# A four-layer block on one core: rebuilt prologue, one-tile statistics, reordered quantised expert

## What is computed

```
x = L0_attn_hidden_states                       # 2 x 512 x 512
x = x + LN(_L0_attn_ref(LN(x), ...))            # selective scan (below)
x = x + LN(_L0_ffn_ref(LN(x), ...))             # 4-bit weights, 1376 wide, gate * sigmoid(gate) * up
x = x + LN(_L1_attn_ref(LN(x), ...))            # attention within a token, 32 heads of 16
x = x + LN(_L1_ffn_ref(LN(x), ...))             # mixture of experts with a shared expert

# _L0_attn_ref, D_IN = 1024, N = 16 states, R = 32:
proj = h @ W_in.T; x, gate = proj[..., :D_IN], proj[..., D_IN:]
x = silu(causal_conv4(x) + conv_b)
ts, Bm, Cm = rms-normed parts of x @ W_x.T      # 32, 16, 16
dt = softplus(ts @ W_dt.T + b_dt)
state = state * exp(dt * A) + (dt * x) * B      # per token, channel and state
y = sum(state * C) + x * D
return (y * silu(gate)) @ W_out.T
```

## Time and profile before

| | us |
|---|---|
| median of 3 runs (lowest, highest) | 844.3 (842.31, 845.25) |
| the profiled execution, device time | 844.68 |
| its span in the trace | 842.8 |
| PE busy | 692.8 (82%) |
| DVE busy | 691.4 (82%) |
| POOL busy | 493.8 (59%) |
| ACT busy | 460.0 (55%) |
| mean granted TensorE clock | 0.904 |

### The profile page before, as it was taken

The page is one execution under the profiler, slowest core; times in us unless marked ns, Lnnn a source line. Parts: engine busy times, 40 slices in busy tenths (PEclk is TensorE's granted clock), DMA queues, the critical chain, the costliest instruction groups (busy, mean ns, idle before and its releaser), DMA issues. The chain is left out here.

```text
span 842.8 us, 8287 instructions
## 1 busy us (share of the span) xinstructions
PE 692.8 (82%) x2732; PEld 320.0 (38%) x2732; DVE 691.4 (82%) x700; ACT 460.0 (55%) x772; POOL 493.8 (59%) x258
## 2 busy tenths in 40 slices
PE   5989679998777879366648868997999999999993
PEld 4533123332222323011112223433444546787882
DVE  5779899999999999979999989997265564586668
ACT  3556687797655765856555434765334346323421
POOL 1319999989999999999998920210002005340151
PEclk9999879999968999756858979999999999999998
DMA  9224312331535524533127029870040030000011
GB/s 289 49 74 158 118 37 95 126 124 65 185 103 182 168 75 138 176 124 113 38 100 222 28 76 236 227 210 18 1 150 1 0 100 2 1 0 1 1 51 50
DMA packets 40945, 82.39 MB, mean 98 GB/s; under 512 B 6711, under 2 KB 8160, under 8 KB 40648
## 3 DMA queue, kind: packets, MB, share of 16 engines
q1 hardware_dynamic: 40904, 81.87, 31.0%
HBM read 70.65 MB, written 11.21 MB: 97 GB/s over the span
## 5 line engine op out<-in xcount | busy, mean ns | idle before, releaser
L2142 POOL TENSOR_TENSOR dbu<-rep_du,bc 128x1024 f32<-128x1024 f32 x128 | 299.6, 2366 | 2.3 <-ACT rep_du L1837 1.4
L1708 ACT ACTIVATE psum<-rep_dt,aneg 128x512 f32<-128x512 f32 x256 | 166.2, 682 | 125.2 <-DVE hc L1115 104.8
L1104 DVE TENSOR_TENSOR_SCAN psum<-psum,dbu 128x1024 f32<-128x1024 f32 x87 | 198.8, 2285 | 10.2 <-ACT psum L1708 9.7
L881 PE MATMUL psum<-hc,stk 128*32 128x512 f32 x512 | 87.5, 762 | 58.8 <-POOL hc L2151 30.4
L1115 DVE TENSOR_TENSOR hc<-psum,bc 128x1024 f32<-128x1024 f32 x87 | 106.5, 1224 | 3.4 <-PE psum L881 0.4
L2151 POOL TENSOR_TENSOR hc<-hc,bc 128x1024 f32<-128x1024 f32 x41 | 96.8, 2360 | 8.6 <-DVE hc L1104 8.5
L1104 DVE TENSOR_TENSOR_SCAN hc<-psum,dbu 128x1024 f32<-128x1024 f32 x41 | 93.5, 2281 | 4.7 <-PE psum L881 2.8
L658 PE MATMUL psum<-xf_hi,gu_hi 128*128 128x512 f16 x176 | 67.4, 383 | 1.5 <-ACT sg L1982 1.0
L658 PE MATMUL psum<-xf_hi,gu_lo 128*128 128x512 f16 x176 | 67.2, 382 | 0.0
L658 PE MATMUL psum<-xf_lo,gu_hi 128*128 128x512 f16 x176 | 67.2, 382 | 0.0
L873 PE MATMUL psum<-u,diag 128*32 128x512 f32 x128 | 24.6, 851 | 42.3 <-DVE u L1131 22.9
(11 more groups left out here) (256 smaller groups left out, 1444.5 us busy)
## 6 DMA issues: line engine op xcount, KB each, us to landing
rep_dt<-rep_scratch SPq DMA_DIRECT2D x60, 256.0 KB, 3.3
rep_du<-rep_scratch SPq DMA_DIRECT2D x60, 256.0 KB, 4.2
cw<-c_scratch SPq DMA_DIRECT2D x11, 768.0 KB, 9.4
qw<-qgu_in SPq DMA_DIRECT2D x11, 512.0 KB, 5.3
bc<-bc_scratch SPq DMA_DIRECT2D x16, 256.0 KB, 4.8
...
```

The costliest lines, as they stand in the source:

```text
L881: last = pe.matmul(y_rows(k), stk[:], hc[:, (i + k // 2) % HCS, k % 2, :], start=False, stop=(s == GN - 1))
L1104: dve.tensor_tensor_scan(h, a, dbu[:, i % DBS].rearrange("p e t -> p (e t)"), 0.0, ALU.mult, ALU.add)\
L1708: last = act.activation(psum[:, 2 * (i % 2) + e, :], rep_dt[:, cc % 2, k, :], ACT.Exp, scale=aneg[:, k, c, n:n + 1])
L2142: pool.tensor_tensor(dbu[:, i % DBS], rep_du[:, cc % 2, k:k + 2, :], bc[:, n, :].unsqueeze(1).broadcast_to([P, 2, L]), ALU.mult).then_inc( ...
```

## The change

There are five parts.

1. **Prologue.** PE runs 12 products of the identity with itself as soon as the identity is loaded, 3 after each of the first three turned tiles and 8 after the last; their result is not used. The projection weights `w_x` come in four DMAs and not two. The Silu table is loaded before the first `conv_tap`, the Ln/Exp table before `square`. `ssm_first` stands behind chunks 4, 5 and 6 (three of them) and behind the last chunk (five). `ms_part` stands ahead of both halves of gate 0. dt of chunk 1 goes to PSUM bank 3 (`dt_second`), ACT takes it in two passes (`dt1_log`, `dt1_pos`), and the rest is done in the loop at pair 2 (`second_steps`). Each spread row group of dt * x goes into a PSUM bank of its own; DVE makes the first `dbu` straight from two of them, and POOL starts with pair 1. The statistics `("ssm", 1)` move behind `normed_ssm(0)`, their root to pair 6, and all four tiles are normed on ACT in the loop.
2. **Side work.** Three gates instead of four are done before the loop, and the rest of `SIDE`'s first row moves by one. dt of chunk 2 is made two places later. The partial output product of tile 3 takes 7 channel chunks and not 6, so one is left for after the loop.
3. **Residual statistics** of sequence 0: `sums` one tile per pair at pairs 91 to 94, `squares` one per pair at 95 to 98, the root at 99 (before: two per pair, at 90, 91, 92 and 93, the root at 94).
4. **Quantised expert.** `unpack(1)` stands before the last `take_y`, `unpack(2)` behind `low_weights(1)`, and `add_partial` is interleaved in another way; on ACT the Silu table is loaded first and `high_weights(1)` stands before `whole(2)`. `high_turned` and `low_turned` for sequence 1 stand at the beginning of a chunk. The statistics `("out", 1)` move from the end of chunk 0 to behind `ffn_low(0, 1)`, those of `("ffn", 1)` from the end of chunk 4 to behind `ffn_low(0, 5)`.
5. **Waits.** Since POOL's first `times_b` is gone, all counts of `bmul_done` are one lower.

```diff
-SIDE = {(0, 1): [("gate", 0, 4)], (0, 2): [("gate", 0, 5)], (0, 3): [("gate", 0, 6)],
-        (1, 1): [("gate", 0, 7)], (1, 2): [("tr", "ssm", 1, 0), ("tr", "ssm", 1, 1)],
+SIDE = {(0, 1): [("gate", 0, 3)], (0, 2): [("gate", 0, 4)], (0, 3): [("gate", 0, 5)],
+        (1, 0): [("gate", 0, 6)], (1, 1): [("gate", 0, 7)], (1, 2): [("tr", "ssm", 1, 0), ("tr", "ssm", 1, 1)],
...
-DT_LATE = DC - 2
+DT_LATE = {0: 2, DC - 2: 1}
...
+            def keep_clock(n):
+
+                for _ in range(n):
+                    pe.matmul(psum[:, 0, 0:P], ident[:], ident[:], start=True, stop=True)
+
             pe.wait_ge(ld_ident, 16)
+            keep_clock(12)
             for t in range(NT):
                 turn("ssm", 0, t, xn)
+                keep_clock(3 if t < NT - 1 else 8)
...
+            def dt_second():
+                pe.matmul(psum[:, KH - 1, :], wdt[0:2 * R + 1, P:2 * P], ssmn[0:2 * R + 1, :], start=True, stop=True)\
+                    .then_inc(dt1_ready, 1)
...
-                if c >= 2:
-                    ssm_first(c - 2)
-            ssm_first(DC - 2)
+                if DC - 1 - SSM_EARLY <= c < DC - 1:
+                    ssm_first(c - DC + 1 + SSM_EARLY)
+            for c in range(SSM_EARLY, DC):
+                ssm_first(c)
+            pe.wait_ge(ld_const, 16 * 6)
+            ms_part(0)
             pe.wait_ge(ld_wg, 16)
             pe.wait_ge(xT_ready, 1)
             gate_half(0, 0, 0)
-            ssm_first(DC - 1)
-            pe.wait_ge(ld_const, 16 * 6)
-            ms_part(0)
             gate_half(0, 0, 1)
...
             dt_part(0)
-            dt_part(1)
-            gate_half(0, 1, 0)
+            dt_second()
             pe.wait_ge(sel_ready, 1)
             wait_taken(pe, ("dt", 0))
-            spread_half(dt_t, 0)
-            spread_half(dt_t, 1)
+            spread_dt_half(0)
             pe.wait_ge(du0_ready, 1)
-            for h in range(2):
-                pe.wait_ge(spread_dt[h], 2)
-                spread_half(du_t, h)
-            gate_half(0, 1, 1)
-            for c in range(2, GATES_FIRST):
+            spread_one(du_t, 0, psum[:, Y_BANK, :])
+            for k in range(1, KH):
+                spread_du(k)
+            pe.wait_ge(dt1_taken, 1)
+            spread_dt_half(1)
+            for c in range(1, GATES_FIRST):
                 gate_part(0, c)
...
+            dve.wait_ge(spread_done, 1)
+            dve.tensor_copy(rep_dt[:, 0, 1, 1:], psum[:, 1, 1:]).then_inc(spread_dt[0], 1)
+
+            wait_work(dve, ("spread", 1))
+            dve.wait_ge(ld_b[0][0], 16)
+            dve.tensor_tensor(dbu[:, 0], psum[:, Y_BANK:Y_BANK + 2, :],
+                              bc[:, 0, :].unsqueeze(1).broadcast_to([P, 2, L]), ALU.mult).then_inc(first_dbu, 1)
+
+            def second_steps():
+
+                dve.wait_ge(sp_ready, 2)
+                dve.wait_ge(spread_done, 2)
+                dve.tensor_tensor(dt_t[:], dt1_log[:], dt1_pos[:], ALU.add).then_inc(dt1_sum, 1)
+                dve.wait_ge(dt1_sum, 1)
+                wait_work(dve, ("spread", KH - 1))
+                dve.tensor_tensor(du_t[:], dt_t[:], u0[:, 1, :], ALU.mult).then_inc(dut_ready, 1)
...
             unpack(0)
+            unpack(1)
             take_y(NCH - 1)
...
-            unpack(1)
             scaled(0)
             add_partial(0)
+            low_weights(0)
             add_partial(1)
-            low_weights(0)
+            scaled(1)
             add_partial(2)
-            unpack(2)
-            scaled(1)
             add_partial(3)
             low_weights(1)
+            unpack(2)
             for i in range(IC):
+                if i > TURN_FIRST:
+                    low_turned(1, [i - TURN_FIRST - 1])
                 ffn_times(0, i)
...
                 ffn_low(0, i)
+                if i == 1:
+                    for t in range(NT):
+                        wait_taken(dve, ("out", 1, t))
+                    stats(("out", 1), [obuf[1][:, t, :] for t in range(NT)])
+                if i == 5:
+                    dve.wait_ge(out_done, NB * NT)
+                    stats(("ffn", 1), x_tiles(1))
...
+            spread_dt_copy(0)
+            decay(0)
+            spread_du_copy(2)
+            spread_du_copy(3)
+            spread_dt_copy(2)
+            spread_dt_copy(3)
+            decay(1)
+            act.wait_ge(first_dbu, 1)
+            act.copy(rep_du[:, 0, 0, :], psum[:, Y_BANK, :])
+            spread_du_copy(1)
...
-                if i in (last + 12, last + 13):
-                    sums(2 * (i - last - 12))
-                    sums(2 * (i - last - 12) + 1)
...
+                if last + 13 <= i < last + 13 + NT:
+                    sums(i - last - 13)
+                if last + 17 <= i < last + 17 + NT:
```

More of the change, by code:

```diff
@@ L113, in pe_order @@
     items = [("tr", "ssm", 0, t) for t in range(NT)] + [("x", 0, c) for c in range(DC)]
-    items += [("ms", 0), ("gate", 0, 0), ("dt", 0), ("dt", 1), ("gate", 0, 1)]
-    items += [("gate", 0, c) for c in range(2, GATES_FIRST)]
+    items += [("ms", 0), ("gate", 0, 0), ("dt", 0)] + [("spread", k) for k in range(1, KH)]
+    items += [("gate", 0, c) for c in range(1, GATES_FIRST)]
     for cc in range(NCH):
@@ L339, in build @@
         ld_z = sem("ld_z")
-        ld_wx = [sem(f"ld_wx{h}") for h in range(2)]
+        ld_wx = [sem(f"ld_wx{h}") for h in range(4)]
         ld_wg = sem("ld_wg")
@@ L380, in build @@
         spread_dt = [sem(f"spread_dt{h}") for h in range(2)]
-        spread_du = [sem(f"spread_du{h}") for h in range(2)]
+        first_dbu = sem("first_dbu")
+        dt1_ready = sem("dt1_ready")
+        dt1_taken = sem("dt1_taken")
+        dt1_sum = sem("dt1_sum")
         reset_done = sem("reset_done")
@@ L752, in out_partial @@
                 item = ("part", t)
-                pe.wait_ge(y_taken, DC + PARTS)
+                pe.wait_ge(y_taken, DC + parts_of(t))
                 start(item)
-                product(item, [(u0[:, c, t * P:(t + 1) * P], wout[:, c, :]) for c in range(PARTS)])\
+                product(item, [(u0[:, c, t * P:(t + 1) * P], wout[:, c, :]) for c in range(parts_of(t))])\
                     .then_inc(work_ready, 1)
@@ L762, in out_part @@
                 product(item, [(gated[b][:, c, t * P:(t + 1) * P], wout[:, c, :])
-                               for c in range(PARTS * b, DC)])\
+                               for c in range(parts_of(t) * b, DC)])\
                     .then_inc(work_ready, 1)
@@ L1829, in _, with spread_dt_copy, spread_du_copy @@
             sp_log(0)
-            for h in range(2):
-                act.wait_ge(spread_done, h + 1)
-                act.copy(rep_dt[:, 0, 2 * h + 1, :], psum[:, 2 * h + 1, :]).then_inc(spread_dt[h], 1)
-            sp_abs(1)
-            sp_exp(1)
-            for h in range(2):
-                act.wait_ge(spread_done, h + 3)
-                act.copy(rep_du[:, 0, 2 * h + 1, :], psum[:, 2 * h + 1, :]).then_inc(spread_du[h], 1)
-            sp_log(1)
+            act.wait_ge(dt1_ready, 1)
+            link(act.activation(dt1_log[:], psum[:, KH - 1, :], ACT.Abs))
+            act.activation(dt1_pos[:], psum[:, KH - 1, :], ACT.Relu).then_inc(dt1_taken, 1)
+            def spread_dt_copy(k):
+                act.wait_ge(spread_done, k // 2 + 1)
+                act.copy(rep_dt[:, 0, k, 1:], psum[:, k, 1:]).then_inc(spread_dt[k // 2], 1)
+            def spread_du_copy(k):
+                item = ("spread", k)
+                wait_work(act, item)
+                act.copy(rep_du[:, 0, k, :], bank(item)).then_inc(taken_sem(item), 1)
             act.wait_ge(a_ready, 2)
```

152 lines of the change are left out of this document (77 added, 75 removed).

## The result

| | before | after |
|---|---|---|
| median, us (lowest, highest) | 844.41 (842.31, 845.25) | 831.44 (830.25, 831.95) |
| span in the trace, us | 842.8 | 828.8 |
| mean granted TensorE clock | 0.904 | 0.909 |

The changed kernel takes 0.9852 of the time of before, 95% interval 0.9838 to 0.9865: 13.0 us less between the medians. 19.2 were forecast. The time lies above the 819.5 to 830 that the prediction calls its forecast, and inside the wider 819.5 to 833, which was to take in rivals A and B as well. Outside the trace lie about 2.2 us in every kernel with the new prologue and about 1.9 in the others, so 0.4 us of the span's gain are missing in the time; why was not looked into. First the stages, with columns and boundaries as in the earlier trace rows; the first scan is now at 57.72 and the first pass of the quantised expert ends at 593.53.

The account below looks back on a forecast made before the run. The prologue is a chain, DVE and POOL nearly bound the loop, PE leads the expert. Savings of 6.8 + 2.4 + 10.0 = 19.2 us gave 825.2; forecast 819.5 to 830, wider range 819.5 to 833.

Parts of the forecast that it names:

- rival A: Prologue: PE's clock stays low during the turns, so fills only delay; first chunk 6.1 us later, 831.3 us; chance 0.10.
- B: Quantised expert: waits change place, so the 4.4 us and the clock's 1.6 are not won; 831.2 us; chance 0.10.
- Prologue: Up to the first scan: last conv 6.1 us earlier, then 14.5 us to the first scan, which starts 9.2 us earlier.
- What the loop takes back: Loop's start up to scan 3: of the 9.2 us head start 6.8 are left, and POOL follows.
- The term for `second_steps`: Loop, ahead of scan 3: two DVE operations at 0.69 us each and hops, 1.5 us.
- signs of being wrong: First scan gains under 7 us, POOL shows new idle time in the loop, or the rest is not 235 us.
- Rival E: Whole kernel: head start lost in the loop since POOL sets its end, expert's waits return; 843 to 845; chance 0.02.
- Statistics one tile per pair: Loop, residual statistics: ACT's and DVE's waits go, POOL is next late, scan 93 gains only 1.7; 2.4 us.
- The expert: Quantised expert's first pass: PE 3.6 us ahead at chunk 8, then 6.4 from the turned tiles; 10.0 us in all.
- (c): Expert, second turned tile: PE's wait falls from 4.40 to 0.6 us and its clock stays high; 4.0 + 2.1, and 0.3.
- step (a): Expert's start: seventh partial chunk saves two of 16 output passes, DVE's new order brings `down(0)` 0.9 us earlier.
- the 826.6 of the drain: Prologue, table load before Square: a 1.38 us drain per switch would end Square 1.4 us later, time 826.6.

Follow-up runs that it names:

- the second trace: The changed kernel run once more with nothing altered, as a measure for other runs; median 831.7 us, 0.9860 of the kernel before.
- after_free_second: The changed kernel with both `second_steps` operations at pair 2 replaced by a 2-column memset, leaving out part of the result; 833.2 us, ratio 0.9878.
- before_turned: The kernel before with only sequence 1's turned halves moved to the beginning of a chunk on ACT and DVE; 837.1 us, ratio 0.9912.

## Why the prediction was right, and what in it was wrong

**The number: inside the range, partly by luck.** 831.4 is 6.2 us above the 825.2 that was said. It is also what rivals A (831.3) and B (831.2) name, and neither came: the first chunk starts at 14.32 (A: 20.3), and PE waits 0.33 us ahead of the second turned tile at the high clock. The range reaches 833 because of these two; what filled it was a miss in the loop for which it was not made.

**Prologue: right.** The last conv ends 5.4 us earlier (6.1 forecast), from there to the first scan 14.52 us (14.5 forecast), together 8.44 for 9.2. But hardly by the fills, whose failure rival A put at 6.1 us: in the kernel before the low stretch ended at 18.5 in the trace and cost ten products 0.2 us each. (The clock column of the earlier trace rows reads 1.00 there all the same; only the pitch of the products shows this stretch.) Most of the 5.4 so has to come from the order of `ssm_first` and the loads, which no run took apart.

**What the loop takes back: wrong, and this is the miss.** The step was "Of 9.2 us 6.8 are left"; 0.65 were, and 0.05 in the second trace. Two things failed. The term for `second_steps` was 1.5 and measured 4.5, by the exclusion of DVE and POOL. Then the sum ended at scan 3 and took it for granted that the rest of the loop follows. after_free_second shows that repairing the first changes nothing: scan 3 at 7.51, scan 17 at 0.13. One of the prediction's own signs of being wrong came with it, new idle time of POOL in the loop: 4.7 us up to scan 8, where before it had none. The places behind scan 3, each seen in a trace: PE's and ACT's work ahead of scan 8, the operation at pair 9, the ring ahead of scan 17, the clock ahead of scan 21. Rival E said "the chain's head start is lost in the loop" and had 0.02, tied to the expert's failure and to POOL as the cause; its first half came true by itself, with the waits pointing at PE and ACT.

**Statistics one tile per pair: right in the loop.** 2.41 us (2.4 forecast), in the shape forecast: scans 92 to 94 no longer wait for ACT, and scan 93 waits for POOL.

```profile
370.92 2.29 DVE L1140 TENSOR_TENSOR_SCAN psum<-psum,dbu 128x1024 f32<-128x1024 f32 x1
376.82 2.29 DVE L1140 TENSOR_TENSOR_SCAN hc<-psum,dbu 128x1024 f32<-128x1024 f32 x1 [2.36 <-POOL dbu L2205]
```

Scan 93 gained 1.6 over scan 91 (1.7 forecast). That all of it reaches the end held in the changed kernel and not in the kernel before, where it was lost to the clock.

**The expert: right, somewhat small.** By chunk 8 3.56 us (3.6 forecast); from there 7.35 (6.4 forecast); together 10.9 (10.0). The sum of (c) has a slip: 4.40 less 0.60 is 3.8 and not 4.0, so it comes to 6.2, as the expectation for before_turned has it.

```profile
508.59 0.69 DVE L1344 TENSOR_TENSOR it<-sg,psum 128x512 f32<-128x512 f32 x1 [2.03 <-ACT sg L2040]
...
593.53 2.05 ACT L2053 CAST y<-psum 128x512 f16<-128x512 f32 x4 [2.00 <-PE psum L939]
```

The first `ffn_times` (508.59) gained only 0.5 us beyond the loop's 3.1, since it waits 2.03 us for silu; but `down(0)`, of which step (a) speaks, starts at 513.61 instead of 517.93, 1.2 us beyond the loop's (0.9 forecast). `down(1)` and `down(5)` wait no more. The table load ahead of Square took 1.28 us and the pass behind it began at once, so the 826.6 of the drain is out:

```profile
43.23 0.63 ACT L1685 ACTIVATE u<-u 128x512 f32<-128x512 f32 x1 [1.87 <-DVE u L1116]
43.88 1.28 ACT L1861 ACT_TABLE_LOAD   x1
45.17 0.59 ACT L1691 ACTIVATE sq<-psum 64x512 f32<-64x512 f32 x1
```

**The sum**: 0.65 + 2.4 + 10.9 = 14.0 of span, 13.0 of the median (11.6 in the second set of runs). Measured part by part it does not add up that neatly: 0 + 0 + 9.1 us alone, 11.8 to 12.5 together. The 3 us between are covered only if all three intervals stand at their upper ends (0.7, 1.1 and 10.9 us); that part 3 lasts only beside part 4 (which takes away the long wait behind which the clock fell) fits, but was not shown.
